# Second norm and pick of six experts in a transformer block: order of the gate's products, of the squares and of the pick

## The reference, cut to what matters

```python
x = x + ao                                   # attention's output, added per head in the kernel
h = rmsnorm(x, ln2_w)                        # second norm: mean of squares, rsqrt, weight
logits = t @ gate_w.T                        # t = h, 2048 tokens; 16 experts
probs = softmax(logits)
topv, topi = top_k(probs, 6)
topv = topv / sum(topv)
routed = sum over the six of  weight * (silu(t @ eg.T) * (t @ eu.T)) @ ed.T
shared = silu(t @ sg_w.T) * (t @ su_w.T) @ sd_w.T      # width 704
out = x + routed + shared
```

## Time and profile before

| | us |
|---|---|
| median of 3 runs | 2202.98 (2201.76 to 2204.27) |
| profiled execution | 2204.81, span 2203.0 |
| TensorE busy | 2125.8 (96%) |
| VectorE busy | 1145.1 (52%) |
| GpSimd busy | 961.7 (44%) |
| ScalarE busy | 721.2 (33%) |
| granted TensorE clock, mean | 0.986 |

### The profile page before, as it was taken

The page is one execution under the profiler, slowest core; times in us unless marked ns, Lnnn a source line. Parts: engine busy times, 40 slices in busy tenths (PEclk is TensorE's granted clock), DMA queues, the critical chain, the costliest instruction groups (busy, mean ns, idle before and its releaser), DMA issues. The chain is left out here.

```text
span 2203.0 us, 39665 instructions
## 1 busy us (share of the span) xinstructions
PE 2125.8 (96%) x11850; PEld 1856.1 (84%) x11851; DVE 1145.1 (52%) x2520; ACT 721.2 (33%) x1896; POOL 961.7 (44%) x1004
## 2 busy tenths in 40 slices
PE   7899999999999999999997899989999999999996
PEld 6788888988888898888886677689999999999996
DVE  6746556464656646465565676633333333333332
ACT  6634344343433434343344122212222222222221
POOL 2535454545545454454521314434444444444442
PEclk9999999999999999999998999999999999999998
DMA  3214333443434344343425211176766766677443
GB/s 110 91 59 170 122 138 125 152 152 114 162 122 140 119 157 157 114 155 122 148 73 199 98 67 48 46 252 161 221 177 175 196 187 161 158 213 187 81 76 53
DMA packets 140690, 300.62 MB, mean 136 GB/s; under 512 B 16800, under 2 KB 16800, under 8 KB 138592
## 3 DMA queue, kind: packets, MB, share of 16 engines
q1 hardware_dynamic: 115392, 241.26, 31.2%
q0 software_dynamic: 24960, 58.21, 13.9%
q10 hardware_dynamic: 288, 0.53, 0.1%
HBM read 177.51 MB, written 122.42 MB: 136 GB/s over the span
## 5 line engine op out<-in xcount | busy, mean ns | idle before, releaser
L753 POOL TENSOR_TENSOR chunk_hi<-chunk_raw,zero 128x512 fp32r<-128x512 f32 x153 | 159.3, 1041 | 238.6 <-DMA chunk_raw<-in_whole 238.6
L1641 POOL DMA_INDIRECT out<-y,sidx x111 | 177.4, 1598 | 65.4 <-issue 43.8
L978 DVE TENSOR_TENSOR pT_lo<-ps,pT_hi 128x384 fp32r<-128x384 f32 (+2 forms) x256 | 111.2, 455 | 176.7 <-ACT pT_hi L914 172.6
L755 POOL TENSOR_TENSOR chunk_raw<-chunk_raw,chunk_hi 128x512 fp32r<-128x512 f32 x153 | 197.7, 1292 | 12.0
L1788 DVE TENSOR_TENSOR prod<-ps,silu 128x352 f32<-128x352 f32 x111 | 58.2, 525 | 271.1 <-PE ps L69 242.2
L951 DVE SCALAR_TENSOR_TENSOR HS<-ps,rinv,HS 128x512 f32<-128x512 f32 x260 | 176.4, 738 | 1.2 <-PE ps L69 1.2
L1648 POOL TENSOR_TENSOR carry<-ident 128x1 f32<-128x1 f32 x214 | 43.3, 203 | 298.7 <-DVE gidx L1794 199.6
L900 ACT ACTIVATE prob<-ps,negmax 128x512 f32<-128x512 f32 (+3 forms) x256 | 131.7, 527 | 110.1 <-DVE negmax L940 110.1
L1783 DVE TENSOR_SCALAR y<-ps,weight_of 128x512 f32<-128x512 f32 x111 | 83.3, 751 | 133.4 <-PE ps L69 127.8
L67 PE MATMUL ps<-ring,xT_0hi 128*128 x448 | 150.3, 336 | 0.8 <-DMA ring<-split_weights 0.8
L67 PE MATMUL ps<-wv_or_qk_hi,hT_hi 128*128 128x256 f32 x512 | 146.8, 287 | 2.9 <-PEq L134 2.9
(11 more groups left out here) (324 smaller groups left out, 6004.1 us busy)
## 6 DMA issues: line engine op xcount, KB each, us to landing
ring<-split_weights SPq DMA_DIRECT2D x240, 272.0 KB
chunk_raw<-in_whole SPq DMA_DIRECT2D x153, 256.0 KB, 2.6
split_weights<-chunk_hi SPq DMA_DIRECT2D x153, 256.0 KB, 2.4
split_weights<-chunk_raw SPq DMA_DIRECT2D x153, 256.0 KB, 2.6
xg<-in_wqk SPq DMA_DIRECT2D x16, 512.0 KB, 3.5
x_spill<-x SPq DMA_DIRECT2D x4, 1024.0 KB, 3.8
xg<-in_wv SPq DMA_DIRECT2D x8, 512.0 KB, 3.5
xg<-in_wo SPq DMA_DIRECT2D x8, 512.0 KB, 4.9
```

The costliest lines, as they stand in the source:

```text
L753: nc.gpsimd.tensor_tensor(chunk_hi[k][:], chunk_raw[k][:], zero[:].to_broadcast([P, CH]), ALU.add).then_inc(chunk_high, 1)
L755: nc.gpsimd.tensor_tensor(chunk_raw[k][:].bitcast(F32R), chunk_raw[k][:], chunk_hi[k][:].bitcast(F32), ALU.subtract).then_inc(chunk_low, 1)
L978: nc.vector.tensor_tensor(pT[1][:, 0:split, w], ps_t[k % 2][:, 0:split * P].rearrange("p (j t) -> p j t", t=P), pT[0][:, 0:split, w].bitca ...
L1641: nc.gpsimd.indirect_dma_start(out, bass.IndirectOffsetOnAxis(ap=sidx[q][:], axis=0), y[q][:], None, bounds_check=T + P - 1, oob_is_err=Tr ...
```

## The change

The squares of batch 1 are issued in the last step of the last pair, in front of ScalarE's wait for the products with v; batch 2 stays behind the last output copy. In the norm stage ScalarE splits the gate before its first tile and VectorE makes the gate's low part right behind the first four norms; VectorE's norms of the next batch are halved around the low tiles of this one. The 12 logits matmuls of a batch are ordered by part: four high by high, four with the low part of the gate, and only then the wait for the low tiles and the four with those. In the shared expert `pick` is cut in four functions, which are issued behind the low parts of chunks 0, 1, 2 of step 0 and chunk 0 of step 1, where before all stood behind chunk 2 of step 0.

```diff
@@ self_attention, scalar @@
                     if more:
                         of_qk(1, 2 * n + 4)
+                    if last and s == STEPS - 1:
+                        squares_of(1)
                     act.wait_ge(pe_o, ONE + n + 1)
                     nc.scalar.copy(oT[0][:], ps_o[:]).then_inc(act_o, 1)
...
             pair(HP - 1, last=True)
-            for b in range(1, NB - 1):
-                squares_of(b)
+            squares_of(NB - 2)
@@ normed_again, tensor @@
             def expert_logits(b):
-                pe.wait_ge(dve_t, ST * (b + 1))
+                def products(w, h, start, stop):
+                    for c in range(DC):
+                        last = nc.tensor.matmul(ps_l[:], gate_s[w][:, c, :], hT[h][:, c, b * S:(b + 1) * S],
+                                                start=start and c == 0, stop=stop and c == DC - 1)
+                    return last
+
+                if b:
+                    pe.wait_ge(act_l, b)
+                else:
+                    pe.wait_ge(act_g, 1)
+                pe.wait_ge(act_t, ST * (b + 1))
+                products(0, 0, True, False)
                 if b == 0:
                     pe.wait_ge(dve_g, 1)
-                else:
-                    pe.wait_ge(act_l, b)
-                for c in range(DC):
-                    last = matmul3(nc, ps_l[:], [w[:, c, :] for w in gate_s],
-                                   [h[:, c, b * S:(b + 1) * S] for h in hT], c == 0, c == DC - 1)
-                last.then_inc(pe_l, 1)
+                products(1, 0, False, False)
+                pe.wait_ge(dve_t, ST * (b + 1))
+                products(0, 1, False, True).then_inc(pe_l, 1)
@@ normed_again, scalar @@
-            high_tiles(0)
             act.wait_ge(ld_g, 16)
             nc.scalar.copy(gate_s[0][:], gate[:]).then_inc(act_g, 1)
+            high_tiles(0)
@@ normed_again, vector (normed takes a range of tiles) @@
             normed(0)
-            normed(1)
-            low_tiles(0)
             dve.wait_ge(act_g, 1)
             nc.vector.tensor_tensor(gate_s[1][:], gate[:], gate_s[0][:].bitcast(F32), ALU.subtract).then_inc(dve_g, 1)
-            for b in range(1, NB):
+            for b in range(NB):
                 if b < LAST:
-                    normed(b + 1)
+                    normed(b + 1, range(2))
                 low_tiles(b)
+                if b < LAST:
+                    normed(b + 1, range(2, ST))
@@ shared_expert, vector @@
-            def pick():
+            def sixth_largest():
 
                 dve.wait_ge(act_e, 1)
                 for t in range(TT):
...
                 step(nc.vector.tensor_tensor(sel[:], ex[:], sixth, ALU.is_gt))
                 step(nc.vector.tensor_tensor(tmp[:], ex[:], sixth, ALU.is_equal))
+
+            def rank_equals():
+
                 step(nc.vector.tensor_reduce(cnt[:], sel[:], AX.X, ALU.add))
                 step(nc.vector.tensor_scalar(cnt[:], cnt[:], -1.0, float(TOPK), ALU.mult, ALU.add))
-                equal = running(acc[0][:], acc[1][:], tmp[:], 2, E)
+                return running(acc[0][:], acc[1][:], tmp[:], 2, E)
+
+            def pick(equal):
+
                 step(nc.vector.tensor_tensor(pos[:], equal, wide(cnt[:]), ALU.is_le))
                 step(nc.vector.tensor_tensor(tmp[:], tmp[:], pos[:], ALU.mult))
                 step(nc.vector.tensor_tensor(sel[:], sel[:], tmp[:], ALU.add))
                 nc.vector.tensor_copy(sel16[:], sel[:]).then_inc(dve_r, 1)
+
+            def weights_of_picked():
+
...
-                    if (n, c) == (2, 0):
+                    if (n, c) == (0, 0):
+                        sixth_largest()
+                    elif (n, c) == (0, 1):
+                        equal = rank_equals()
+                    elif (n, c) == (0, 2):
+                        pick(equal)
+                    elif (n, c) == (1, 0):
+                        weights_of_picked()
+                    elif (n, c) == (2, 0):
                         ends = place(total)
...
-                if n == 0:
-                    pick()
-                elif n == 1:
+                if n == 1:
                     total = count_tokens()
```

More of the change, by code:

```diff
@@ L1107, in _, with normed @@
         def _(dve):
-            def normed(b):
+            def normed(b, some=range(ST)):
                 dve.wait_ge(pool_r, b + 1)
-                for i in range(ST):
+                for i in some:
                     k = ST * b + i
```

## The result

The changed kernel takes 2190.93 us (median of 6, 2189.30 to 2195.67) against 2203.62 (6 runs of before), ratio 0.9949 with a 95% interval of 0.9939 to 0.9959, that is 9 to 13 us faster. A second set of runs gives 2192.67 against 2202.96, ratio 0.9950 (0.9937 to 0.9964). The forecast was 2192.3 and 10.7 us faster. Three executions far off all others (2671 and 4197 us of two later versions, 6521 us of before) are left out of every median and ratio here.

A forecast was written before the change was run, and what follows sets the result against it. TensorE, busy 96% of the span, was taken as the bound, so only its idle stretches, low-clock stretches and barriers could give time. Terms 3.0 + 5.0 + 2.7 = 10.7 us put the median at 2192.3, range 2187 to 2198.

The forecast's parts named there:

- Part 1: End of attention: batch 1's squares fit ScalarE's idle hole, so the stage ends 3.0 us earlier; bounds 0 to 3.3.
- the output copy isn't late: Last attention step: four squarings, 3.04 us, fit ScalarE's 3.74 us hole before the last output copy.
- Part 2: Norm stage: reordering without removing work shortens it from a reckoned 31.7 to 26.5 us; 5.0 taken of 5.2.
- my upper bound of 5.6: Norm stage: gain if TensorE has no low clock level at all, the stage then taking 26.1 us.
- ScalarE's tile 14: Norm stage: stands behind the third logits copy, stopping VectorE 1.4 us before low tile 15, which ends at 22.5.
- rival C: End of norm stage passes to the DMA: last store lands at 29, total gain 8.2 us, 2194.8; chance 0.08.
- Part 3: Shared expert: pick in pieces turns TensorE's 7.6 us stop into one of 5.1 before the fifth chunk; gain 2.7 us.
- Rivals A and B: Shared expert: A, pieces hidden whole, 2186.1, chance 0.07; B, port starves VectorE until the adds end, 2197.1, chance 0.11.
- The sum: Whole kernel: 3.0 + 5.0 + 2.7 = 10.7 us faster, median 2192.3.
- Rival D: Norm stage: TensorE stays at its lower clock throughout, stage 40 us, kernel 2.8 us slower, 2205.8; chance 0.02.

The follow-up runs named there:

- without part 1: Changed kernel with GpSimd's x1 adds held until the six are picked, squares of batches 1 and 2 both behind the last output copy: 2188.56 us, ratio 0.9933.
- the first trace: First profiled execution of the changed kernel, no further edit: span 2187.3 us.
- the second trace: Changed kernel run and profiled once more with no edit: median 2192.67 us, ratio 0.9950 to the kernel before.
- the part alone: Kernel before with only the pick cut in four pieces at their four places: 2200.21 us, ratio 0.9985.
- The late adds: Changed kernel with one added wait, GpSimd's 16 adds of x1 start when the six are picked: 2186.69 us, ratio 0.9917.
- part 1 alone: Kernel before with only batch 1's squares moved into the last attention step: 2201.82 us, ratio 0.9993.

## Why the prediction was right

**Part 1, 3.0 us.** The mechanism was right, squares in ScalarE's hole and GpSimd's root off the end; the size holds for the upper and the mixed clock only (2.7 and 2.8) and is 1.2 to 1.4 where the output products are slow. The step that failed in detail is "the output copy isn't late": the hole of 3.74 us was one of an execution in which the products with v ran slow (0.56 granted, 1159.3 to 1162.7). At the upper clock it is 2.44 us (ScalarE's idle in front of the copy without part 1), less than the 3.04 of the squares, and the copy starts behind them.

**Part 2, 5.0 us.** The stage took 25.3 us where the reckoning gave 26.5; the gain was 6.2 to 6.3, past my upper bound of 5.6. The clock isn't what I had wrong, though in the first trace nothing in the stage ran low, where I had let the first transposes run low to 5 us: without any low level I had reckoned 26.1, still 0.8 too long, and in the second trace the transposes did run low (0.60 granted, 1168.7 to 1173.0) and the stage took 25.3 us all the same. TensorE's row of that trace, against the 2.65 and 1.32 us of the first:

```profile
1168.68 4.57 PE L1050 MATMUL ps<-ident,norm 128*128 128x128 f32 x24 [1.98 <-DVE norm L1121]
```

The mis-sized term is how late ScalarE's tile 14 comes: VectorE stops 1.4 us for it in the reckoning and 0.16 in the trace. Low tiles 7 and 11 ended where they were reckoned (12.1 and 17.1 us against 12.2 and 17.3), low tile 15 at 21.1 and not 22.5, and the last logits began at 20.4 us and not 21.7. These 1.3 us account for the 1.2 between 26.5 and 25.3. The last store, issued by 1185.74 and waited for 3.8 us, landed 22.7 us into the stage (forecast 22.5), 2.3 us ahead of the barrier in place of 8.8: rival C didn't come, but its margin is now small. Which half carries the gain I hadn't asked; the greater one is the products' order (4.4 us alone).

**Part 3, 2.7 us.** 3.1 to 3.7 in the traces of the whole change and of the part alone. The wait was where it was forecast and 4.0 us long, not 5.1. Piece two took 11.8 us in the first trace (1206.29 to 1218.04), as reckoned (11.9); what was 0.7 us early, counted from the barrier, was its start. The first compare ran free since the adds began 9.7 us behind the barrier in place of 9.0, and low part 1 took 1.18 in place of 1.67. Rivals A and B are out: the pieces paid the adds, each operation one add and not two. The late adds show that GpSimd's adds are the cause and price them at 5.6 us still in the changed kernel (39.6 to 33.9). The rule of the Trainium skill's page "SBUF — State Buffer", section "Who interferes with whom", agrees with these runs: with two inputs in SBUF the add of 240 elements took 1.44 us beside GpSimd's adds and 0.41 without them.

**The sum.** 10.7 forecast; the two ratios give 11.2 and 11.0, the medians 12.7 and 10.3. Of the 15.7 us between the two first spans 4.0, 6.3 and 3.6 lie in the three stretches, 0.5 ahead of them and 1.4 behind them. Of the 4.0 at the end of attention 2.8 are part 1 and 1.2 the clock (18.4 us with part 1 alone under the clock of before, 17.2 here). Where the output products run slow the three parts are 1.2 to 1.4, 6.2 and 3.1, 10.5 to 10.7 in all. That the total came so near is in part luck: parts 2 and 3 gave about 1.2 and 0.4 to 0.9 us more than forecast, and part 1 up to 1.8 less. Rival D, the lower clock through the whole stage, didn't come: it lasted 4.3 us in the second trace.

## What to carry to other kernels

When VectorE's small operations all take one length whatever their size, look at what GpSimd does beside them before cutting the work in pieces: moving GpSimd's adds behind the pick gave 8.4 us with one wait, the four pieces 3.6. In split products, issue the terms that need only the early part first and wait for the late part last; that alone gave 4.4 us of a 31.5 us stage. Read the size of a hole at both levels of TensorE's clock: a hole behind slow matmuls (3.7 us) is smaller when they run fast (2.4).

## What the runs showed that I had not expected

The same kernel's end of attention took 17.2 or 20.4 us, by which of two groups of products the lower clock met; executions of one kernel differ by up to 7 us in all (before 2200.5 to 2207.4), more than one part of this change gives. And a wait of 4.0 us cost TensorE the lower clock (0.55 granted behind it) much like the one of 7.6 did (0.50), so halving a stop doesn't save that part of its price; removing it does.
